# Half of a dense expert stage placed inside the second half of a four-layer recurrence, in a single-core Trainium2 kernel

## The chip, the core and the metric

The kernel runs on one core of a Trainium2 chip. The core has five engines that run side by side, each with its own program: TensorE (matmuls, written PE in the rows; PEld is its weight load), VectorE (DVE), ScalarE (ACT), GpSimd (POOL) and SyncE (SP, which here only issues DMAs). They meet only through semaphores: an instruction can wait for a count and raise one when it ends. SBUF is the working memory (128 partitions), PSUM the small memory into which TensorE writes; it has eight banks of 128x512 fp32. The metric is the time of one execution on the device, in microseconds (us); lower is better.

## The reference

All arithmetic is fp32. The tokens are 32 sequences of 128 tokens with 128 features. In short:

```python
# adapter: 10 languages, one per sequence, two small matrices, LayerNorm
x_a = layernorm(x + relu(x @ W1[id] + b1[id]) @ W2[id] + b2[id]) * gamma[id] + beta[id]
# four layers of a selective state space model, 256 channels, 16 states each
for layer in range(4):
    xs, z = split(layernorm(h) @ W_in.T)                 # 2 x 256 channels
    u = silu(causal_conv4(xs))
    dt, B, C = split(u @ W_x.T)                          # 8, 16, 16
    dt = softplus(dt @ W_dt.T + b_dt)
    for t in range(128):                                 # per channel and state
        H = exp(dt[t] * A) * H + dt[t] * B[t] * u[t]
        y[t] = sum over 16 states of H * C[t]
    h = h + ((y + u * Dp) * silu(z)) @ W_out.T
x1 = x + h
# dense stage: 8 weighted experts and one shared one, all of them for all tokens
dense = sum over 9 experts of w[e] * (silu(x1 @ Wg[e]) * (x1 @ Wu[e])) @ Wd[e]
# sparse stage: router, top 2 of 8, fixed capacity, gelu experts
out = x1 + sum of top-2 gate * expert(dense)
```

## The kernel before

The program has four phases that follow one another: `setup_phase` (adapter, weights), `mamba_phase` (the recurrence), `dense_phase` and `sparse_phase`. The change is about the second and third.

**Tiling of the recurrence.** Four sequences form a group (512 tokens); there are 8 groups and 4 layers. One group in one layer is called an *item* here; the 32 items are run layer by layer, all 8 groups in each. The 256 channels are two halves of 128 partitions, and the 16 states are worked two at a time, so that an item has 16 *steps* (8 pairs of states for each half). A step is a chain over four engines:

- ScalarE, `decay`, L543: two `exp` of 128x508 write a buffer `dA` (four of them);
- VectorE, `input_term`, L592: the product `psdB<-psU,Bt` of 128x1024, with `psU` (dt times u) in PSUM and `Bt` (the rows of B spread over the partitions) in SBUF, the result in one of two PSUM buffers;
- VectorE, `scan_step`, L598: the scan along time of 128x1024, `hh<-dA,psdB`, one input in SBUF and one in PSUM;
- GpSimd, `gg<-hh,Ct`, L683: the product with C of 128x1024, both inputs in SBUF;
- TensorE, `sum_states`, L385: two identity matmuls of 512 columns that add the two states to `psY`.

Beside the steps each engine's program has, at step numbers fixed by hand in the tables `PE_AT`, `ACT_AT`, `DVE_AT` and `POOL_AT`, the preparation of the next item and the finish of the one before: projections, convolution and time step (PE L416 to L429, ACT L486 to L517), `dt` and `dtu` on GpSimd (L653, L658, 128x1024 each), ScalarE's copies of `dtu` into `psU` (L522), the gates `yg` (GpSimd L668, 128x512 twice), the residual (GpSimd L664), and the LayerNorm statistics (VectorE L606 to L612, GpSimd L643 to L648).

**What sets the order.** Every engine runs its program in order. A scan may run four steps ahead of GpSimd (`NHB`), GpSimd four ahead of TensorE (`NGB`), the exps four ahead of the scan (`NDA`), the input terms one ahead of the scan (`NDB` is 2). PSUM is full: two buffers of two banks for the input term, two banks `psU`, one `psY`, one `psW` for all projections.

**The dense stage**, 8 groups one after another, has 36 rounds per group (9 experts, 4 pieces of the hidden layer). A round is three matmuls of 512 columns (L897, L901, L866), a Silu on ScalarE (L948) and a product on VectorE (L1051, one input in PSUM). GpSimd scales the input once per expert (L811). The input of a group is x + h, added on VectorE from two SBUF tensors (`residual`, L980). Router logits and slots of group g are computed inside group g+1.

## Time and profile before

| | us |
|---|---|
| three timed runs: median | 2933.65 |
| lowest and highest | 2931.76, 2934.94 |
| the profiled execution: its time | 2935.85 |
| its span, first to last instruction | 2934.1 |
| TensorE busy | 2515.8 (86%) |
| VectorE busy | 2104.9 (72%) |
| GpSimd busy | 1780.1 (61%) |
| ScalarE busy | 1456.5 (50%) |

The shares are averages over stages that have different limits, so they say little by themselves. A timeline row gives the start, the duration, engine, line, operation, output and inputs, and in brackets how long the engine had been idle before and who released it. Records of one matmul of 512 fp32 columns come in pairs (two records, one matmul).

### The profile page before, as it was taken

To read this page: it belongs to the slowest core of one execution; us is meant where nothing else is said; L and a number is where in the kernel's file an instruction comes from. 1 tells how busy PE (TensorE), PEld (TensorE's weight loads), DVE (VectorE), ACT (ScalarE), POOL (GpSimd) and SP (SyncE) were. 2 spreads that over 40 slices of the span, in tenths; PEclk is the share of its full clock that TensorE was granted. 3 is DMA by queue.
4 is the path that set the end of the run, shared out by engine and by line. 5 is a ranking of instruction groups with operands and counts; after the bars stand their busy time and mean duration, and the time that the engine had idled before them with its cause. 6 is when DMAs were issued, how large, how long until landed. Compare 5 with 4: busy or idle time off the path is not lost. (4 is left out here: it accounts for less than half of the span.)

```text
span 2934.1 us, 27727 instructions
## 1 busy us (share of the span) xinstructions
PE 2515.8 (86%) x6470; PEld 1112.9 (38%) x6470; DVE 2104.9 (72%) x2075; ACT 1456.5 (50%) x2337; POOL 1780.1 (61%) x1090
## 2 busy tenths in 40 slices
PE   5588888888888888888888888869999999999586
PEld 3233333333333333333333333324444444444264
DVE  4399999999999999999999999972333333333221
ACT  2366657666666665666566667632222222222222
POOL 3278887888888788888888887861022202221266
PEclk9798999999999999989999999999999999999798
DMA  7334533543453344345434533516000000000154
GB/s 204 139 128 179 201 127 144 194 170 127 170 197 139 136 185 186 127 157 196 154 128 174 205 127 142 195 61 220 8 15 8 15 7 11 25 8 1 45 111 70
DMA packets 130514, 354.33 MB, mean 121 GB/s; under 512 B 21716, under 2 KB 85410, under 8 KB 97570
## 3 DMA queue, kind: packets, MB, share of 16 engines
q1 hardware_dynamic: 116770, 342.46, 32.1%
q0 software_dynamic: 11264, 7.98, 1.8%
q10 hardware_dynamic: 2432, 3.38, 0.3%
q14 instruction: 34, 0.28, 0.0%
q8 instruction: 14, 0.23, 0.0%
HBM read 330.34 MB, written 23.99 MB: 121 GB/s over the span
## 5 line engine op out<-in xcount | busy, mean ns | idle before, releaser
L683 POOL TENSOR_TENSOR gg<-hh,Ct 128x1024 f32<-128x1024 f32 x512 | 1205.0, 2356 | 336.2 <-DVE hh L598 322.4
L598 DVE TENSOR_TENSOR_SCAN hh<-dA,psdB 128x1024 f32<-128x1024 f32 x512 | 1170.7, 2287 | 59.4 <-ACT dA L543 6.1
L385 PE MATMUL psY<-gg,ident 128*128 128x512 f32 x2048 | 1024.4, 636 | 128.0 <-POOL gg L683 127.7
L543 ACT ACTIVATE dA<-dt,Acur 128x508 f32<-128x508 f32 x1024 | 664.6, 707 | 14.9 <-DVE hh L598 14.4
L385 PEld LDWEIGHTS psY<-gg,ident 128*128 128x128 f32 x2048 | 390.9, 200 | 689.8 <-issue 420.6
L592 DVE TENSOR_TENSOR psdB<-psU,Bt 128x1024 f32<-128x1024 f32 x512 | 617.6, 1206 | 36.8 <-ACT psU L522 36.8
L1051 DVE TENSOR_TENSOR ac<-sg,d_bank 128x512 f32<-128x512 f32 x288 | 198.1, 688 | 514.0 <-PE d_bank L901 496.8
L948 ACT ACTIVATE sg<-d_bank 128x512 f32<-128x512 f32 x288 | 171.9, 597 | 534.6 <-PE d_bank L897 521.3
L811 POOL TENSOR_TENSOR xw<-x1T,wbc 128x512 f32<-128x512 f32 x72 | 74.9, 1041 | 568.1 <-PE d_bank L901 563.8
L897 PE MATMUL d_bank<-x1T,wgu 128*128 128x512 f32 x576 | 296.6, 597 | 1.9 <-DMA wgu<-in_Wu 1.9
L901 PE MATMUL d_bank<-xw,wgu 128*128 128x512 f32 x576 | 295.5, 595 | 0.0
L866 PE MATMUL d_bank<-ac,wdn 128*128 128x512 f32 x576 | 291.7, 593 | 0.0
L416 PE MATMUL psW<-xnT,wcur 128*128 128x512 f32 x512 | 235.9, 603 | 3.9 <-DMA diag<-diags_l 2.1
L493 ACT ACTIVATE u<-psW,parc 128x512 f32<-128x512 f32 x64 | 44.0, 687 | 240.1 <-PE psW L416 240.1
L901 PEld LDWEIGHTS d_bank<-xw,wgu 128*128 128x128 f32 x576 | 110.3, 191 | 138.6 <-issue 124.0
L866 PEld LDWEIGHTS d_bank<-ac,wdn 128*128 128x128 f32 x576 | 109.7, 190 | 137.5 <-issue 137.5
L897 PEld LDWEIGHTS d_bank<-x1T,wgu 128*128 128x128 f32 x576 | 108.5, 191 | 130.0 <-issue 130.0
L380 PE MATMUL psY<-u,diag 128*128 128x512 f32 x128 | 86.1, 760 | 74.0 <-ACT yg L528 74.0
L416 PEld LDWEIGHTS psW<-xnT,wcur 128*128 128x128 f32 x512 | 98.5, 193 | 131.4 <-issue 119.0
L429 PE MATMUL psW<-xd,wdcur 8*128 8x512 f32 x128 | 87.2, 766 | 63.5 <-ACT soft L511 43.4
L1127 POOL DMA_INDIRECT out<-eos,home x64 | 99.2, 1549 | 69.1 <-DVE eos L1219 50.2
L821 POOL DMA_INDIRECT disp<-tok,idx x64 | 62.5, 976 | 77.0 <-DVE idx L1029 50.3
...
## 6 DMA issues: line engine op xcount, KB each, us to landing
Bt<-rows SPq DMA_DIRECT2D x128, 1024.0 KB, 6.0
Ct<-rows SPq DMA_DIRECT2D x128, 1024.0 KB, 4.7
...
```

Of the source, the lines that this page charges most:

```text
L385: ins = pe.matmul(psY[:, :], lhsT=ident[:, :], rhs=gg[k % NGB][:, j, :], start=False, stop=(k % NK == NK - 1 and j == 1))
L416: ins = pe.matmul(psW[:, :], lhsT=wcur[:, k, c * 128:(c + 1) * 128], rhs=xnT[:, :, k:k + T], start=(k == 0), stop=(k == NTAP - 1))
L543: ins = act.activation(dA[k % NDA][:, j, :, 1:T], dt[p][:, c, :, 1:T], ACT.Exp, scale=Acur[p][:, s:s + 1])
L592: dve.tensor_tensor(dB[k % NDB][:, :, :], psU[c][:, :].unsqueeze(1).broadcast_to([128, 2, TOK]), Bt[:, s:s + 2, :], ALU.mult).then_inc(dbu, 1)
L598: dve.tensor_tensor_scan(out=hh[k % NHB][:, :, :].rearrange("p c t -> p (c t)"), data0=dA[k % NDA][:, :, :, :].rearrange("p c q t -> p (c ...
L683: pool.tensor_tensor(gg[k % NGB][:, :, :], hh[k % NHB][:, :, :], Ct[:, s:s + 2, :], ALU.mult).then_inc(prod, 1)
L866: ins = pe.matmul(psD[:, :], lhsT=wdn[:, r // NF, r % NF, :], rhs=ac[r % NAC][:, :], start=(r == 0), stop=(r == NST - 1))
L897: pe.matmul(psG[r % 2][:, :], lhsT=wgu[:, e, 0, f * 128:(f + 1) * 128], rhs=x1T[p][:, :, :], start=True, stop=True).then_inc(gated, 1)
L901: pe.matmul(psU[r % 2][:, :], lhsT=wgu[:, e, 1, f * 128:(f + 1) * 128], rhs=xw[(NE1 * p + e) % NXW][:, :, :], start=True, stop=True).then_ ...
L948: act.activation(sg[r % NSG][:, :], psG[r % 2][:, :], ACT.Silu).then_inc(silued, 1)
L1051: dve.tensor_tensor(ac[r % NAC][:, :], sg[r % NSG][:, :], psU[r % 2][:, :], ALU.mult).then_inc(acted, 1)
L1127: pool.indirect_dma_start(tokens, bass.IndirectOffsetOnAxis(ap=home[p][:, n:n + 1], axis=0), eos[p][:, n, :], None, bounds_check=NSEQ * T ...
```

## The change

The recurrence and the first half of the dense stage become one phase, `wave_phase`, written out without a hardware loop.

- **Order of items.** The first 16 items take groups 0 to 3 through all four layers, the last 16 take groups 4 to 7 (`layer`, `group`). From item 15 (`FIRST`) on, the dense stage of groups 0 to 3 is run inside the steps, nine rounds to an item: `G_AT`, `U_AT` and `D_AT` hold the steps at which TensorE issues the gate, up and down matmul of each; ScalarE copies a gate four or five steps later (`place_gate`) and runs the Silus together (`silu_gates`); VectorE's product follows the scan two steps behind the up matmul (`act_product`). TensorE transposes x1, GpSimd adds x and scales the inputs (`add_x`, `scale`).
- **Steps by pairs of states.** A step now alternates between the two halves of the channels for the same pair of states. `psY` has two banks, one for each half; the sums are copied and gated once per item as 128x1024.
- **PSUM.** The `psU` banks are gone: VectorE's input term reads `dtu` from SBUF. From item 14 on only one of the two input-term buffers is used as such (`dB[0]`); the other holds the gate and up results of the dense stage. The dense sum has a bank.
- **Input terms from GpSimd.** In items 0 to 13, GpSimd makes the input term of steps 4, 9 and 13 (`GIVEN`, `give`), and ScalarE moves it to PSUM (`move_given`).
- **Sums.** `PAIRED` is empty: TensorE adds all sixteen states. The residual is one more identity matmul in `out_projection`.
- The rest of the dense stage, groups 4 to 7, follows in `dense_phase`; the router's work for all 8 groups is done there, two groups in each (`posts`), as is the last group's at the end. The dispatch buffers are cleared early in the recurrence. `sparse_phase` keeps its work.

VectorE's program. Names ending in a digit are buffers; `psU0` is PSUM, `dtu0` and `Bt` are SBUF, `f_sg` is the Silu in SBUF. In the kernel before, two steps of the first item:

```order
L592 TENSOR_TENSOR psdB0<-psU0,Bt 128x1024 [waits m_scan,m_b_ld2]
L598 SCALAR_TENSOR_TENSOR hh0<-dA0,psdB0 128x1024 [waits m_prod,m_dbu,m_da]
L592 TENSOR_TENSOR psdB1<-psU0,Bt 128x1024 [waits m_scan]
L598 SCALAR_TENSOR_TENSOR hh1<-dA1,psdB1 128x1024 [waits m_prod,m_dbu,m_da]
L606 BN_STATS stats<-h_res 128x6 [waits m_moments]
```

And in the changed kernel, a stretch of an item in the second half:

```order
L730 TENSOR_TENSOR psdB0<-dtu0,Bt 128x1024 [waits m_scan,m_b_ld3]
L741 SCALAR_TENSOR_TENSOR hh2<-dA2,psdB0 128x1024 [waits m_prod,m_dbu,m_da]
L762 TENSOR_TENSOR f_ac0<-f_sg,psdB1 128x512 [waits m_downed,m_upped,m_sg_ok]
L730 TENSOR_TENSOR psdB0<-dtu0,Bt 128x1024 [waits m_scan]
L741 SCALAR_TENSOR_TENSOR hh3<-dA3,psdB0 128x1024 [waits m_prod,m_dbu,m_da]
L730 TENSOR_TENSOR psdB0<-dtu0,Bt 128x1024 [waits m_scan,m_b_ld0]
L741 SCALAR_TENSOR_TENSOR hh0<-dA0,psdB0 128x1024 [waits m_prod,m_dbu,m_da]
L762 TENSOR_TENSOR f_ac1<-f_sg,psdB1 128x512 [waits m_downed,m_upped,m_sg_ok]
```

The input term has both inputs in SBUF and always the same output buffer, so that its wait on `m_scan` is for the scan just before it; nine times per item a product of the dense stage stands between a scan and the next input term.

GpSimd's program in the first half. In the kernel before, the first eleven steps of the first item:

```order
L683 TENSOR_TENSOR gg<-hh,Ct 128x1024 x7
L643 TENSOR_TENSOR vare<-mv,eps 128x4
L644 TENSOR_SCALAR negm<-mv 128x4
L646 TENSOR_TENSOR rstd<-vare,nhalf 128x4
L648 TENSOR_TENSOR nmr<-negm,rstd 128x4
L683 TENSOR_TENSOR gg<-hh,Ct 128x1024 x4
```

In the changed kernel, the same eleven steps:

```order
L818 TENSOR_TENSOR gg<-hh,Ct 128x1024
L810 TENSOR_TENSOR f_sg<-dtu,Bt 128x1024
L818 TENSOR_TENSOR gg<-hh,Ct 128x1024 x5
L810 TENSOR_TENSOR f_sg<-dtu,Bt 128x1024
L818 TENSOR_TENSOR gg<-hh,Ct 128x1024
L784 TENSOR_TENSOR vare<-mv,eps 128x4
L785 TENSOR_SCALAR negm<-mv 128x4
L787 TENSOR_TENSOR rstd<-vare,nhalf 128x4
L789 TENSOR_TENSOR nmr<-negm,rstd 128x4
L818 TENSOR_TENSOR gg<-hh,Ct 128x1024 x2
L810 TENSOR_TENSOR f_sg<-dtu,Bt 128x1024
L818 TENSOR_TENSOR gg<-hh,Ct 128x1024 x2
```

Three products of 128x1024 (`f_sg<-dtu,Bt`) have come to GpSimd in each item.

On TensorE, twenty-seven matmuls of 512 columns of the dense stage stand among the sums and projections of an item of the second half.

The diff, cut to its core:

```diff
-NK = NS // 2
-NSTEP = NH * NK
-NCK, CKS = 4, NS // 4
+NSTEP = NS
+ROUND = NG // 2
+NB = NE1
+NDF = NG // 2
+FIRST = NL * ROUND - 1
...
+GIVEN = {4: 0, 9: 5, 13: 8}
+POOL_AT = {3: ["gate"], 6: ["rstd"], 10: ["dt"], 11: ["dtu"]}
+G_AT = [-9, -8, -6, -5, -4, -3, -2, -1, 3]
+U_AT = [6, 8, 9, 11, 12, 14, 15, 19, 20]
+D_AT = [10, 10, 11, 13, 14, 18, 18, 21, 22]
+PAIRED = []
...
+def layer(t):
+    return t // ROUND % NL
+def group(t):
+    return t // (NL * ROUND) * ROUND + t % ROUND
+def stream(at, i, k):
+    return [NB * v + m for v in range(NDF * NF) for m in range(NB) if NSTEP * (FIRST + v) + at[m] == NSTEP * i + k]
...
-        psU = [ctx.enter_context(nc.psum_tensor(f"psU{c}", [128, TOK], f32)) for c in range(NH)]
-        psY = ctx.enter_context(nc.psum_tensor("psY", [128, TOK], f32))
+        psG, psU = dB[1][:, 0, :], dB[1][:, 1, :]
+        psY = ps("psY", [128, NH, TOK])
+        psD = ps("psD", [128, TOK])
...
                 def input_term(i, k):
-                    n, c, s = NSTEP * i + k, k // NK, 2 * (k % NK)
...
-                    at_least(dve, scan, CR + n + 1 - NDB)
-                    dve.tensor_tensor(dB[k % NDB][:, :, :], psU[c][:, :].unsqueeze(1).broadcast_to([128, 2, TOK]), Bt[:, s:s + 2, :], ALU.mult).then_inc(dbu, 1)
+                    n, c, s = NSTEP * i + k, k % NH, k // NH
...
+                    if assisted(i, k):
+                        return
+                    b, free = (k % NDB, n + 1 - NDB) if i < FIRST - 1 else (0, n)
+                    at_least(dve, scan, free)
+                    dve.tensor_tensor(dB[b][:, :, :], dtu[i % 2][:, c, :].unsqueeze(1).broadcast_to([128, 2, TOK]), Bt[:, s % NPR, :, :], ALU.mult).then_inc(dbu, 1)
...
+                def act_product(n):
+                    dve.wait_ge(sg_ok, n // NB + 1)
+                    dve.wait_ge(upped, n + 1)
+                    at_least(dve, downed, n - 1)
+                    dve.tensor_tensor(ac[n % 2][:, :], sg[:, n % NSLG, :], psU, ALU.mult).then_inc(acted, 1)
...
+                        input_term(i, k)
+                        scan_step(i, k)
+                        for n in stream([a + 2 for a in U_AT], i, k):
+                            act_product(n)
...
+                def give(i, k):
...
+                    pool.tensor_tensor(given[helped(n) % 2], dtu[i % 2][:, c, :].unsqueeze(1).broadcast_to([128, 2, TOK]), Bt[:, s % NPR, :, :], ALU.mult).then_inc(gave, 1)
...
+                def move_given(i, k):
...
+                    act.activation(dB[k % NDB][:, :, :], given[helped(n) % 2], ACT.Copy).then_inc(moved, 1)
...
+                def place_gate(n):
+                    act.wait_ge(gated, use_g(n) + 1)
...
+                    act.activation(sg[:, n % NSLG, :], psG, ACT.Copy).then_inc(gfree, 1)
...
+                def gate(n):
...
+                    pe.wait_ge(gfree, use_g(n))
+                    pe.matmul(psG, lhsT=fwg[:, e % NXW, f * 128:(f + 1) * 128], rhs=flat(n // NST), start=True, stop=True).then_inc(gated, 1)
...
+                def up(n):
...
+                    at_least(pe, acted, n)
+                    pe.matmul(psU, lhsT=fwu[:, e % NXW, f * 128:(f + 1) * 128], rhs=xw[:, e % NXW, :, :].rearrange("p q t -> p (q t)"), start=True, stop=True).then_inc(upped, 1)
+                def down(n):
...
+                    pe.wait_ge(acted, n + 1)
...
+                    pe.matmul(psW[:, :], lhsT=ident[:, :], rhs=flat(group(t)), start=True, stop=False)
...
+                def scale(a):
+                    d, e = a // NE1, a % NE1
+                    pool.wait_ge(gfree, use_t(d) + 1)
+                    at_least(pool, upped, NF * (a - NXW + 1))
+                    pool.tensor_tensor(xw[:, e % NXW, :, :], residents(d), wbc[:, e, G * d:G * (d + 1)].unsqueeze(2).broadcast_to([128, G, T]), ALU.mult).then_inc(scaled, 1)
```

## Rows read from the trace of the kernel before

**Rows 1.** Windows: busy us of each engine (count), TensorE clock, DMA, by phase
```profile
core 0: us, PE busy (x) PEld busy (x) DVE busy (x) ACT busy (x) POOL busy (x), PEclk, DMA share, GB/s
123.25:1965.46 1842.21, 1558.30 (x3657) 634.86 (x3658) 1781.44 (x1303) 1173.30 (x1863) 1501.77 (x791) 0.93 0.42 159
1965.46:2740.00 774.54, 764.13 (x1891) 347.77 (x1890) 243.09 (x508) 204.83 (x333) 136.29 (x167) 0.99 0.10 32
2740.00:2934.10 194.10, 130.15 (x726) 92.63 (x724) 40.03 (x95) 46.02 (x72) 106.93 (x72) 0.87 0.44 83
```

**Rows 2.** Costliest groups by line, with shape: busy us, mean ns, idle before
```profile
L683 POOL TENSOR_TENSOR gg<-hh,Ct 128x1024 f32<-128x1024 f32 x512 | 1205.0, 2356 | 336.2 <-DVE hh L598 322.4 <-PE psY L385 13.8
L598 DVE TENSOR_TENSOR_SCAN hh<-dA,psdB 128x1024 f32<-128x1024 f32 x512 | 1170.7, 2287 | 59.4 <-ACT dA L543 6.1 <-DVE psdB L592 5.9 <-POOL gg L683 5.5
L592 DVE TENSOR_TENSOR psdB<-psU,Bt 128x1024 f32<-128x1024 f32 x512 | 617.6, 1206 | 36.8 <-ACT psU L522 36.8
L980 DVE TENSOR_TENSOR x1g<-xin,h_res 128x512 f32<-128x512 f32 x8 | 7.5, 936 | 3.2 <-DMA xin<-in_x 3.2
```

**Rows 3.** Timeline of VectorE, two steps in the middle of the recurrence
```profile
998.61 2.29 DVE L598 TENSOR_TENSOR_SCAN hh<-dA,psdB 128x1024 f32<-128x1024 f32 x1
1000.81 1.21 DVE L592 TENSOR_TENSOR psdB<-psU,Bt 128x1024 f32<-128x1024 f32 x1
1002.11 2.29 DVE L598 TENSOR_TENSOR_SCAN hh<-dA,psdB 128x1024 f32<-128x1024 f32 x1
```

**Rows 4.** Timeline of GpSimd: `deviation`, a step beside rows 3, back-to-back work
```profile
329.30 0.20 POOL L643 TENSOR_TENSOR vare<-mv,eps 128x4 f32<-128x4 f32 x1
...
331.03 2.36 POOL L683 TENSOR_TENSOR gg<-hh,Ct 128x1024 f32<-128x1024 f32 x1
...
1001.05 2.35 POOL L683 TENSOR_TENSOR gg<-hh,Ct 128x1024 f32<-128x1024 f32 x1 [1.15 <-DVE hh L598]
...
1030.15 2.35 POOL L683 TENSOR_TENSOR gg<-hh,Ct 128x1024 f32<-128x1024 f32 x1 [1.14 <-DVE hh L598]
1032.46 2.35 POOL L653 TENSOR_TENSOR dt<-dt,soft 128x1024 f32<-128x1024 f32 x1
```

**Rows 5.** Timeline: the residual add on VectorE, GpSimd idle, then GpSimd busy
```profile
1977.89 0.69 DVE L980 TENSOR_TENSOR x1g<-xin,h_res 128x512 f32<-128x512 f32 x1 [3.17 <-DMA xin<-in_x]
...
2085.77 1.04 POOL L811 TENSOR_TENSOR xw<-x1T,wbc 128x512 f32<-128x512 f32 x1 [9.26 <-PE d_bank L901]
2085.78 0.69 DVE L1051 TENSOR_TENSOR ac<-sg,d_bank 128x512 f32<-128x512 f32 x1 [1.78 <-PE d_bank L901]
2086.39 0.97 DVE L980 TENSOR_TENSOR x1g<-xin,h_res 128x512 f32<-128x512 f32 x1
```

**Rows 6.** Timeline of the setup: a VectorE product between two GpSimd products
```profile
17.55 0.72 POOL L167 TENSOR_TENSOR taps<-wraw,cwb 128x256 f32<-128x256 f32 x1
17.65 0.89 DVE L216 TENSOR_TENSOR wbc<-wbc 128x256 f32<-128x256 f32 x1
18.23 0.90 POOL L167 TENSOR_TENSOR taps<-wraw,cwb 128x256 f32<-128x256 f32 x1
```

**Rows 7.** Timeline of the setup: VectorE beside back-to-back GpSimd products
```profile
26.19 1.40 POOL L167 TENSOR_TENSOR taps<-wraw,cwb 128x256 f32<-128x256 f32 x2
26.33 1.46 DVE L235 SCALAR_TENSOR_TENSOR ad_nrm<-ad_y,ad_mv,ad_gb 128x128 f32<-128x128 f32 x1
```

**Rows 8.** Timeline of the setup: VectorE beside GpSimd's power on four elements
```profile
55.74 0.62 DVE L235 SCALAR_TENSOR_TENSOR ad_nrm<-ad_y,ad_mv,ad_gb 128x128 f32<-128x128 f32 x2
55.76 1.01 POOL L174 TENSOR_TENSOR ad_rstd<-ad_vare,nhalf 128x4 f32<-128x4 f32 x1
```

**Rows 9.** Windows: one item of the recurrence, one group of the dense stage
```profile
1000.00:1057.60 57.60, 50.67 (x118) 20.76 (x117) 55.83 (x42) 37.06 (x59) 47.31 (x25) 0.91 0.42 161
2086.39:2181.25 94.86, 94.86 (x237) 43.24 (x236) 30.97 (x68) 25.84 (x42) 17.37 (x18) 1.00 0.04 12
```

**Rows 10.** Timeline of TensorE late in the dense stage: two matmuls
```profile
2734.57 1.02 PE L897 MATMUL d_bank<-x1T,wgu 128*128 128x512 f32 x2
2735.43 1.02 PE L901 MATMUL d_bank<-xw,wgu 128*128 128x512 f32 x2
```

More of the change, by code:

```diff
@@ new lines, in wave_phase @@
+        fwg = sb("f_wg", [128, NXW, F])
+        fwu = sb("f_wu", [128, NXW, F])
+        fwd = sb("f_wd", [128, NXW, NF, D])
+        xw = sb("f_xw", [128, NXW, G, T])
+        xin = sb("f_xin", [128, G, D])
+        ac = [sb(f"f_ac{b}", [128, TOK]) for b in range(2)]
+        given = [sg[:, 2 * b:2 * b + 2, :] for b in range(2)]
+        zrow = sg[:, 4:7, :].rearrange("p s t -> p (s t)")[:, 0:NCH * RW]
+        dB = [ps(f"psdB{b}", [128, 2, TOK]) for b in range(NDB)]
+        psG, psU = dB[1][:, 0, :], dB[1][:, 1, :]
@@ L318, in at_least, with assisted, helped, residents @@
+        b_ld, c_ld = ([sem(f"{n}_ld{j}") for j in range(NPR)] for n in "bc")
+        g_ld, ud_ld = ([sem(f"{n}_ld{j}") for j in range(NXW)] for n in ("fg", "fud"))
+        W = psw_uses()
+        def assisted(i, k):
+            return i < FIRST - 1 and k in GIVEN
+        def helped(n):
+            return sum(assisted(a // NSTEP, a % NSTEP) for a in range(n))
         def at_least(eng, sm, v):
-            if not (isinstance(v, int) and v <= CR):
+            if v > 0:
                 eng.wait_ge(sm, v)
+        def residents(d):
+            return h_res[:, G * d:G * (d + 1), :]
@@ new lines, in sum_states, with out_projection @@
+                def sum_states(i, k):
+                    n = NSTEP * i + k
+                    pe.wait_ge(prod, n + 1)
+                    last = 1 if i >= FIRST and k in PAIRED else 2
+                    for j in range(last):
+                        ins = pe.matmul(psY[:, k % NH, :], lhsT=ident[:, :], rhs=gg[k % NGB][:, j, :], start=False, stop=(k >= NSTEP - NH and j == last - 1))
+                    ins.then_inc(red, 1)
+                def out_projection(t):
+                    pe.wait_ge(ygated, t + 1)
+                    pe.wait_ge(wfree, W["out", t])
+                    pe.matmul(psW[:, :], lhsT=ident[:, :], rhs=flat(group(t)), start=True, stop=False)
@@ L454, in last, with transpose_x @@
                     for q in range(G):
                         for c in range(NH):
-                            ins = pe.matmul(psW[:, q * T:(q + 1) * T], lhsT=yg[1][:, c, q * T:(q + 1) * T], rhs=wo[:, (NL - 1) * NH + c, :], start=(c == 0), stop=(c == NH - 1))
+                            ins = pe.matmul(psW[:, q * T:(q + 1) * T], lhsT=yg[:, c, q * T:(q + 1) * T], rhs=wo[:, layer(t) * NH + c, :], start=False, stop=(q == G - 1 and c == NH - 1))
                     ins.then_inc(wready, 1)
-                loop(pe, body, first, last)
+                def transpose_x(d):
+                    pe.wait_ge(x1_ok, d + 1)
+                    if d == 0:
+                        pe.wait_ge(scan, NSTEP * (FIRST - 1))
+                    at_least(pe, gfree, use_t(d))
+                    for q in range(G):
+                        ins = pe.transpose(psG[:, q * T:(q + 1) * T], h_res[:, G * d + q, :], ident[:, :])
+                    ins.then_inc(gated, 1)
@@ new lines, in down @@
+                def down(n):
+                    e, f = expert(n)
+                    pe.wait_ge(acted, n + 1)
+                    if n % NST == 0:
+                        at_least(pe, sum_ok, n // NST)
+                    pe.matmul(psD[:, :], lhsT=fwd[:, e % NXW, f, :], rhs=ac[n % 2][:, :], start=(n % NST == 0), stop=(n % NST == NST - 1)).then_inc(downed, 1)
+                transposes(0)
+                for k in sorted(PE_AT):
+                    for what in PE_AT[k]:
+                        if what in PRE:
+                            pre(0, what)
@@ L575, in _ @@
+                            if what == "sums" and i > 0:
+                                copy_sums(i - 1)
+                        decay(i, k)
+                copy_sums(NIT - 1)
+                added(NIT - 1)
             @block.vector
             def _(dve):
-                for sm in (dbu, scan, stat, moments):
-                    dve.sem_inc(sm, CR)
                 for b in range(NDA):
                     ins = dve.memset(dA[b][:, :, :, 0:1], 0.0)
-                ins.then_inc(zeroed, 1)
@@ L753, in at_least, with posts, sums @@
                 eng.wait_ge(sm, v)
-        def loop(eng, first, body, last):
-            first()
-            body(0, 0, False, True)
-            with eng.Fori(0, NG // 2 - 1) as j:
-                body(2 * j + 1, 1, True, True)
-                body(2 * j + 2, 0, True, True)
-            body(NG - 1, 1, True, False)
-            last(NG - 1, 1)
+        def posts(h, r, at):
+            return [2 * h + j for j in range(2) if 2 * h + j < NG - 1 and r == P_AT[j] + at]
+        def sums(g):
+            return h_res[:, G * g:G * (g + 1), :]
         with nc.Block() as block:
```

852 lines of the change are left out of this document (451 added, 401 removed).

## The prediction

> **What bounds the kernel now.** I read the windows by phase first, then the groups by line, then the timelines of VectorE and GpSimd inside one step. In the recurrence, 123.25 to 1965.46, 1842.2 us for 32 items or 57.57 us each, VectorE is busy 1781 of 1842 us and GpSimd 1502 [rows 1]. VectorE's share is the sum of two rows of 512 instructions each, the scan with 2.287 us and the input term with 1.206 us [rows 2]. In the timeline a step starts 3.50 us after the last one (998.61 to 1002.11) with no idle between: the input term starts 0.09 us before the scan's recorded end, the next scan 0.09 us behind the input term [rows 3]. 16 steps make 56.0 us; 1.6 us remain for the statistics. GpSimd's product starts 0.15 us after the scan that it needs (scan ends 1000.90, product starts 1001.05) [rows 3, 4]. So VectorE sets the recurrence. The dense stage, 774.5 us, is TensorE's: one group takes 94.86 us with TensorE busy all through [rows 9], 0.86 us per matmul of 512 columns (2734.57 to 2735.43) [rows 10]. What is to be gained is four of eight such groups: 379 us.
>
> **The rows that decide the price.** The input term now reads two tensors in SBUF; before, one of its inputs was in PSUM, as for the scan. What such a VectorE instruction does beside GpSimd the trace shows in three places. (a) The residual add of 128x512, both inputs in SBUF, takes 0.69 us with GpSimd idle. When GpSimd's product of two SBUF tensors is in work (2085.77 to 2086.81), it takes 0.97 us and ends 0.55 us behind GpSimd's end, while GpSimd keeps its 1.04 us [rows 5]. The mean of all eight, 0.936 us [rows 2], is one of 0.69 and seven of 0.97. 512 elements need about 0.52 us of data: 1024 take 1.206 us [rows 2] and 512 take 0.69 [rows 5], which is 1.01 ns per element. So it moved nothing until GpSimd was done. (b) In the setup a product of 256 elements that starts 0.10 us behind a GpSimd product takes 0.89 us where its data need 0.26 us; it ends 0.27 us after that product's end, and the next GpSimd product takes 0.90 instead of 0.72 us [rows 6]. So the second of the two waits in either direction, and GpSimd's loss is the data time less 0.08 us. (c) Once VectorE was passed over: its product of 128 elements waited 1.46 us across the boundary of two back-to-back GpSimd products [rows 7].
>
> The Trainium skill, "SBUF — State Buffer", section "SBUF: two separate sides", says that the port pair shared by VectorE and GpSimd is an exclusive lock, taken by whichever starts first for the whole instruction, and names VectorE instructions with two SBUF inputs. The trace agrees [rows 5, 6]. "For the whole instruction" isn't quite what the trace shows [rows 8]: two VectorE instructions with two SBUF inputs ran at 0.31 us each inside a GpSimd instruction of 1.01 us on four elements. If a GpSimd product lost the whole 1.21 us of each input term and not its data time less 0.08, the sum below would be 45 us longer.
>
> **First half, items 0 to 13.** VectorE saves three input terms: 13 x 3.50 + 3 x 2.20 + 1.6 = 53.7 us without any blocking. GpSimd: 16 products, 3 given input terms, gate, dt and dtu, all 128x1024, 22 x 2.31 us (1030.15 to 1032.46) = 50.8, and 1.73 for the deviation (329.30 to 331.03) [rows 4]: 52.5 us. But each of the 13 input terms stops GpSimd for 1.04 - 0.08 = 0.96 us, together 12.5 us: 65.0 us in which one or the other moves data. The input term is issued ahead of the scan's end and gets in first; the queue of four `hh` buffers lets GpSimd fall behind, then the scans wait for it. I take 66 us; 53.7 if nothing is blocked. 14 items: 924 us.
>
> **Second half, items 15 to 30.** Per step VectorE now waits for its own scan before the input term: 2.29 + 0.09 + 1.21 + 0.09 = 3.68 us instead of 3.50. The dense product (0.69, next start 0.61 later [rows 5]) reads PSUM and SBUF and isn't blocked itself. But it puts the input term 0.61 us behind its place: GpSimd's product, released 0.15 us after the scan, is then in work and holds the port until 0.15 + 2.35 = 2.50 us; the input term's data (1.04, and 0.03 to its end) follow, then 0.09 and the scan: 2.50 + 1.07 + 0.09 + 2.29 = 5.95 us. Nine steps of an item are like that. In the seven others the two are released by the same scan, VectorE after 0.09 us and GpSimd after 0.15; I take it that VectorE gets in first, and GpSimd's product runs beside the next scan. 9 x 5.95 + 7 x 3.68 = 79.3 us. The statistics follow a product step and hide under GpSimd's 2.35. GpSimd's other work fits beside a scan in product steps; the gate after step 3 doesn't, 2.0 us, and about half of the 2.25 scalings per item, 1.5 us together. 82.8; with a little for late up matmuls, 83.5 us. 16 items: 1336.
>
> TensorE in such an item: 50.7 us of busy time now [rows 9] and 27 x 0.86 = 23.2: 73.9 us, under 83.5, so the dense matmuls cost only by the waits that they bring. They are issued behind the sums of their step, two steps ahead of VectorE's product; behind a late one wait the input term and the scan, with 1.9 us of slack, since the input term waits for GpSimd anyhow. ScalarE: 37.1 us [rows 9], nine gate copies and their Silus, about 10: 47. Neither is near.
>
> Item 14 (no dense products, no given terms): 16 x 3.68 + 10 for gate, dt, dtu, statistics and the x add = 69. Item 31: four product steps, 4 x 5.95 + 12 x 3.68 + 2 = 70.
>
> **Rest.** Before the recurrence 123.3, unchanged. Behind it 968.6 now (774.5 + 194.1) [rows 1], less 4 x 94.86, and 4 more posts of the router on TensorE at some 2 us: 597.6. DMAs: the same bytes of B and C in pieces of half the size, with a lead of six steps, over 20 us; the weights of an expert (three loads per 4 rounds) have ten steps. I cost them at nothing; if one came late it would show as a VectorE wait at the first step of a pair.
>
> Sum: 123.3 + 924 + 69 + 1336 + 70 + 597.6 = 3120 of span. The profiled execution was 1.8 us longer than its span and 2.2 above the median, so the median is about the span: 3120. Some passing over as in (c) will happen: I say 3130 us, 196 slower. The recurrence grows by 2399 - 1842 = 557 us to save 371.
>
> **Rivals.**
> 1. *Nothing of weight is blocked.* The input term keeps 1.21 us though both inputs are in SBUF. First half 53.7; second half by VectorE 16 x 3.68 + 1.6 + 9 x 0.61 = 66, by TensorE 67 at full clock to 74: 71. 123.3 + 14 x 53.7 + 62 + 16 x 71 + 62 + 597.6 = 2733. For it: the design, in which GpSimd takes over products, needs it. Against: the seven adds of [rows 2, 5]. 10 in 100.
> 2. *GpSimd gets in first also in the plain steps, or back to back.* The 0.06 us between the releases [rows 3, 4] is smaller than what is unknown of when each asks for the port. Then all steps of the second half take 5.95: 95.2 x 18 = 1714 us for items 14 to 31 instead of 1475, and 3360. If instead it passes VectorE over in the first half as in [rows 7], each of the six extra products costs 4.4 instead of 2.3 us and leaves the port idle under the next scan: 80 instead of 66, and 3330. For: [rows 7]. Against: [rows 6], where VectorE got in. 27 in 100 for 3230 to 3450.
> 3. *Blocking is partial*, or GpSimd is mostly out of the way when the input term comes, because TensorE delays the products past the 2.35 us and GpSimd has finished: nine steps at 4.6 to 5 us, 70 to 75 per item, 2900 to 3040. 13 in 100, a quarter of it below 2928.
> 4. *TensorE decides*: its clock falls in the new waits and 73.9 becomes 90 and more; then VectorE waits in every product step, at 3200 and up. Part of the 27.
>
> The other side begins where the second half's items cost less than 83.5 - 196/16 = 71 us with the first half as forecast: that needs the product steps at 4.6 us.
>
> **How the numbers follow.** Main case 50 in 100, 3040 to 3230; rival 1 10, rival 3 13, rivals 2 and 4 27. The range 2960 to 3400 leaves out rival 1 and the lower half of rival 3, and a few in 100 above. A measurement of this kernel tells 0.2% (6 us) from no change: faster 0.13, within 0.2% 0.01, slower 0.86.
>
> **What would show it.** In the changed profile the rows of `psdB<-dtu,Bt` have a mean well above 1.21 us: near 2 in the first half, 2.5 to 3 behind a dense product. GpSimd's `gg<-hh,Ct` has a mean above 2.6. VectorE's busy share stays near 95% while the step is longer: the wait is inside the instruction and not in front of it. A step of the second half alternates between 3.7 and 5.95 us. The dense group of the last phase stays at some 97 us. It is wrong if `psdB<-dtu,Bt` keeps 1.21 us (rival 1), if no step of the second half is near 3.7 (rival 2), or if VectorE's product waits for the up matmul for over 2 us in most steps (rival 4).

## The result and the profile after

The changed kernel takes 3238.06 us (median of 4 runs, 3236.67 to 3241.4), the kernel before 2933.16 (4 runs beside it): the ratio is 1.1041, 95% interval 1.1022 to 1.106, so it is 305 us slower. Forecast were 3130 us with a range of 2960 to 3400: the sign and the range hold, the size was too small by 108 us. 3238 us is 8 us above the band of the prediction's main case (3040 to 3230), inside the one that it gave to its rivals 2 and 4.

The costliest groups of the changed kernel by line, the same three that stand in [rows 2] (busy us, mean ns, idle time before and its releaser):

```profile
L818 POOL TENSOR_TENSOR gg<-hh,Ct 128x1024 f32<-128x1024 f32 x512 | 1415.8, 2770 | 592.6 <-DVE hh L741 585.2
L741 DVE TENSOR_TENSOR_SCAN hh<-dA,psdB 128x1024 f32<-128x1024 f32 x512 | 1166.0, 2284 | 122.5 <-ACT dA L657 84.4
...
L730 DVE TENSOR_TENSOR psdB<-dtu,Bt 128x1024 f32<-128x1024 f32 x470 | 1087.5, 2314 | 47.4 <-POOL dtu L799 36.1
```

The scan has kept its 2.28 us. The input term has gone from 1206 to 2314 ns and GpSimd's product from 2356 to 2770, with next to no idle time ahead of the input term: the wait stands inside the instruction, and would be read as work. 512 input terms of 1.206 us were 618 us; 470 of 2.314 are 1088.

Windows of the changed kernel by phase, answering to [rows 1] (the stretch and its length, then busy us of PE, PEld, DVE, ACT and POOL with the number of instructions, the granted TensorE clock, the DMA share and GB/s). An item runs from the start of its first scan to the start of the next item's. The rows are: before the recurrence, items 0 to 13, item 14, items 15 to 30, item 31, the dense stage that is left, the sparse stage:

```profile
0.00:121.20 121.20, 61.44 (x196) 37.09 (x196) 40.33 (x170) 34.19 (x74) 36.20 (x62) 0.94 0.57 163
121.20:1077.30 956.10, 746.45 (x1633) 306.14 (x1634) 859.64 (x534) 545.84 (x830) 900.88 (x363) 0.87 0.44 147
1077.30:1154.00 76.70, 60.90 (x133) 24.89 (x132) 74.18 (x42) 38.48 (x61) 59.20 (x24) 0.87 0.42 139
1154.00:2558.70 1404.70, 1200.68 (x2737) 502.33 (x2736) 1338.38 (x788) 717.28 (x1059) 912.84 (x403) 0.94 0.38 126
2558.70:2636.30 77.60, 47.83 (x95) 19.01 (x95) 75.10 (x35) 17.80 (x27) 44.73 (x16) 0.84 0.18 61
2636.30:3041.00 404.70, 396.07 (x1011) 184.09 (x1012) 137.46 (x357) 114.98 (x181) 99.12 (x129) 0.98 0.11 35
3041.00:3236.50 195.50, 132.35 (x731) 93.52 (x729) 40.75 (x96) 46.64 (x73) 106.91 (x72) 0.88 0.43 82
```

The recurrence takes 2515 us (121.2 to 2636.3) where it took 1842; what follows it takes 600.2 where it took 968.6. So 368 us are saved behind the recurrence and 673 are paid in it.

Two timelines of the changed kernel in item 20, VectorE and then GpSimd (start, duration, engine, line, operation; in brackets the idle time before):

```profile
1687.68 0.66 DVE L762 TENSOR_TENSOR f_ac<-f_sg,psdB 128x512 f32<-128x512 f32 x1
1688.26 3.02 DVE L730 TENSOR_TENSOR psdB<-dtu,Bt 128x1024 f32<-128x1024 f32 x1
1691.38 2.29 DVE L741 TENSOR_TENSOR_SCAN hh<-dA,psdB 128x1024 f32<-128x1024 f32 x1
1693.70 1.23 DVE L730 TENSOR_TENSOR psdB<-dtu,Bt 128x1024 f32<-128x1024 f32 x1
1695.02 2.29 DVE L741 TENSOR_TENSOR_SCAN hh<-dA,psdB 128x1024 f32<-128x1024 f32 x1
1697.41 3.42 DVE L730 TENSOR_TENSOR psdB<-dtu,Bt 128x1024 f32<-128x1024 f32 x1
1700.92 2.29 DVE L741 TENSOR_TENSOR_SCAN hh<-dA,psdB 128x1024 f32<-128x1024 f32 x1
```

```profile
1687.84 2.35 POOL L818 TENSOR_TENSOR gg<-hh,Ct 128x1024 f32<-128x1024 f32 x1 [3.54 <-DVE hh L741]
1690.16 2.02 POOL L834 TENSOR_TENSOR f_xw<-h_res,wbc 128x512 f32<-128x512 f32 x1
1693.74 3.39 POOL L818 TENSOR_TENSOR gg<-hh,Ct 128x1024 f32<-128x1024 f32 x1 [1.57 <-DVE hh L741]
1697.39 2.35 POOL L818 TENSOR_TENSOR gg<-hh,Ct 128x1024 f32<-128x1024 f32 x1 [0.25 <-DVE hh L741]
```

All three cases are here. At 1688.26 the input term comes 0.42 us behind GpSimd's product, because the dense product stood in front of it, and takes 3.02 us; it ends 1.1 us behind GpSimd. At 1693.70 it starts 0.03 us behind the scan's end and 0.04 ahead of GpSimd: it takes 1.23 us, and GpSimd's product 3.39. At 1697.41 no product stood in front, and still it starts 0.10 us behind the scan's end (1697.31) and 0.02 behind GpSimd: 3.42 us. Scan to scan the three steps are 5.90, 3.64 and 5.90 us.

The difference between the last two is in the program. The first is the second half of a pair of states and waits for the scan alone (`m_scan`); the other opens a pair and waits for the rows of B as well (`m_scan,m_b_ld`), which had long been there. That wait costs some 0.07 us of start, and 0.07 us decides who gets in first, at 2.26 us of VectorE's time. It is so in the whole stretch of items 14 to 31. Of the input terms that come straight behind a scan, the 64 that wait for the scan alone start 0.02 to 0.04 us after its end, and 55 of them take 1.2 us; the 77 that wait for B as well and have nothing else in front of them start 0.09 to 0.14 us after it, and 67 of them take 3.4 us. Of the sixteen steps of item 20 only two are 3.64 us, one is 4.28 and one 5.61; the other twelve are 5.89 or more, though only nine have a product.

### The profile page after: what moved, and what is told of

Read it like the earlier page. It is cut to its first block and busy times, and to the rows that moved or that the text cites. A ratio compares the mean times of both kernels' runs of the same rounds, so it can differ in the third digit from the quotient of the medians.

```text
span 3236.5 us, 23204 instructions
## 1 busy us (share of the span) xinstructions
PE 2645.7 (82%) x6530; PEld 1167.1 (36%) x6530; DVE 2565.8 (79%) x2019; ACT 1515.2 (47%) x2304; POOL 2159.9 (67%) x1069
## 5 line engine op out<-in xcount | busy, mean ns | idle before, releaser
L818 POOL TENSOR_TENSOR gg<-hh,Ct 128x1024 f32<-128x1024 f32 x512 | 1415.8, 2770 | 592.6 <-DVE hh L741 585.2
L741 DVE TENSOR_TENSOR_SCAN hh<-dA,psdB 128x1024 f32<-128x1024 f32 x512 | 1166.0, 2284 | 122.5 <-ACT dA L657 84.4
L730 DVE TENSOR_TENSOR psdB<-dtu,Bt 128x1024 f32<-128x1024 f32 x470 | 1087.5, 2314 | 47.4 <-POOL dtu L799 36.1
L1206 DVE TENSOR_TENSOR ac<-sg,d_bank 128x512 f32<-128x512 f32 x144 | 99.0, 687 | 243.7 <-PE d_bank L1056 226.6
L483 PE MATMUL psW<-xnT,wcur 128*128 128x512 f32 x512 | 239.6, 611 | 8.3 <-DMA diag<-diags_l 6.5
L1105 ACT ACTIVATE sg<-d_bank 128x512 f32<-128x512 f32 x144 | 86.0, 597 | 261.7 <-PE d_bank L1052 261.6
L538 PE MATMUL psdB<-f_xw,f_wu 128*128 128x512 f32 x288 | 154.4, 618 | 35.3 <-DVE f_ac L762 35.3
L606 ACT ACTIVATE u<-psW,parc 128x512 f32<-128x512 f32 x64 | 44.0, 687 | 258.7 <-PE psW L483 161.7
L530 PE MATMUL psdB<-h_res,f_wg 128*128 128x512 f32 x288 | 161.5, 645 | 0.0
L483 PEld LDWEIGHTS psW<-xnT,wcur 128*128 128x128 f32 x512 | 100.7, 197 | 140.7 <-issue 132.0
L1052 PE MATMUL d_bank<-x1T,wgu 128*128 128x512 f32 x288 | 148.9, 599 | 0.7 <-ACT x1T L1083 0.7
L1056 PE MATMUL d_bank<-xw,wgu 128*128 128x512 f32 x288 | 147.9, 595 | 0.0
L1019 PE MATMUL d_bank<-ac,wdn 128*128 128x512 f32 x288 | 145.8, 592 | 0.0
L545 PE MATMUL psD<-f_ac,f_wd 128*128 128x512 f32 x288 | 143.6, 599 | 0.0
```

Source lines behind the costliest of these rows:

```text
L483: ins = pe.matmul(psW[:, :], lhsT=wcur[:, k, c * 128:(c + 1) * 128], rhs=xnT[:, :, k:k + T], start=(k == 0), stop=(k == NTAP - 1))
L530: pe.matmul(psG, lhsT=fwg[:, e % NXW, f * 128:(f + 1) * 128], rhs=flat(n // NST), start=True, stop=True).then_inc(gated, 1)
L538: pe.matmul(psU, lhsT=fwu[:, e % NXW, f * 128:(f + 1) * 128], rhs=xw[:, e % NXW, :, :].rearrange("p q t -> p (q t)"), start=True, stop=Tru ...
L545: pe.matmul(psD[:, :], lhsT=fwd[:, e % NXW, f, :], rhs=ac[n % 2][:, :], start=(n % NST == 0), stop=(n % NST == NST - 1)).then_inc(downed, 1)
L730: dve.tensor_tensor(dB[b][:, :, :], dtu[i % 2][:, c, :].unsqueeze(1).broadcast_to([128, 2, TOK]), Bt[:, s % NPR, :, :], ALU.mult).then_inc ...
L741: dve.tensor_tensor_scan(out=hh[k % NHB][:, :, :].rearrange("p c t -> p (c t)"), data0=dA[k % NDA][:, :, :, :].rearrange("p c q t -> p (c ...
```

## The experiments

Each runs on one chip beside the kernel before, whose median was 2936.3 to 2936.7 us. The theory under test (A) is that the time goes to the port that VectorE and GpSimd share for operands in SBUF, at a price that the order of arrival sets. The rivals, named in each expectation, are other things that came with the change: TensorE's order, ScalarE's late exps, the waits as such.

**1. The wait for B moved ahead.** The waits for the rows of B and for `dtu` are taken before the scan and not before the input term.

```diff
 def input_term(i, k):
-    if k == 0:
-        dve.wait_ge(dtu_ok, i + 1)
-    if c == 0:
-        dve.wait_ge(b_ld[s % NPR], 16 * (NS // 2 // NPR * i + s // NPR + 1))
...
 def scan_step(i, k):
+    if n + 1 < NSTEP * NIT:
+        inputs_ready((n + 1) // NSTEP, (n + 1) % NSTEP)
```

> Edit: VectorE waits for the piece of B (and, once per item, for dtu) in front of the scan before and no longer at the input term, so that the input term waits for the scan alone. Theory A (whoever asks first gets the shared SBUF port, and a second semaphore makes VectorE 0.07 us later than GpSimd): the plain steps that end ahead of an even-numbered input term and now take 5.90 us fall to 3.64; three per item in the second half, eight of item 14, three of item 31: 16 x 6.8 + 18 + 7 = 130 us less than 3238, 3108. First half unchanged within 1 us per item. Rival B (the steps of 5.90 come from something else, a late exp or a late TensorE): no change, 3238 within 10. Rival C (the wait merely moves its 0.07 us and the order stays): 3238 to 3250.

Measured: 3162.51 us (4 runs), 1.0772 of before [1.0754, 1.079], 76 us less than the changed kernel; theory A had expected some 130. The input term's mean falls to 1999 ns and GpSimd's product rises to 2908. Item 14, which has no dense products, falls from 76.7 to 69.0 us, exactly the forecast that had taken all plain steps as won. An item of the second half falls by 3.6 us only (87.8 to 84.2). The four plain steps ahead of an even-numbered input term are now 3.64 to 3.8 and give back 8.0 us of an item, but one or two steps of each item have become 7.7 to 10.1 us, and the idle time ahead of `f_ac` has grown from 33 to 90 us, 52 of it for `psD`. So the second wait is shown to decide the plain steps; in the second half over half of what they give back is lost again, and 3.6 us of an item are added waits for TensorE.

**2. The dense product moved behind the input term.** The order scan, dense product, input term becomes scan, input term, dense product.

```diff
                         input_term(i, k)
-                        scan_step(i, k)
-                        for n in stream([a + 2 for a in U_AT], i, k):
+                        for n in stream([a + 3 for a in U_AT], i, k):
                             act_product(n)
+                        scan_step(i, k)
```

> Edit: VectorE's product of the dense stage stands behind the next input term and ahead of its scan, and no longer between a scan and the next input term. Theory A (the product gives GpSimd the port first): the nine product steps of an item no longer hand the port to GpSimd by their place; they are then like plain steps, and only those whose input term waits for two semaphores still lose: about 8 x 3.64 + 8 x 5.9 + 9 x 0.6 + 1.2 = 83 us per item instead of 87.8, 3160. Rival B (the product steps are long because the up matmul is late): no gain or slower, since the product is asked for 1.2 us later at best; 3220 to 3260. Rival C (arrival order doesn't matter, VectorE gets in at once): 16 x 3.64 + 6.6 = 65, limited by TensorE at 74: 3238 - 16 x 14 = 3015.

Measured: 3127.53 us (4 runs), 1.0652 [1.0634, 1.067], 110 us less, where 78 were expected. No multiplication, byte or matmul is gone: only the place of nine instructions of 0.69 us per item.

**3. Both.**

> Both edits together. Theory A: all steps of the second half become plain steps that VectorE wins: 16 x 3.64 + 9 x 0.6 + 1.2 = 65 us per item for VectorE, less than the 67 to 74 of TensorE, so TensorE decides: 72 to 76 per item; 3238 - 16 x 14 - 20 for items 14 and 31: 2995 (2960 to 3040). The two gains are more than the sum of each alone (130 and 80). Rival B (TensorE or ScalarE hold the second half at over 83 already): the gain stays under 100 us, over 3130.

Measured: 3042.79 us (4 runs), 1.0366 [1.0348, 1.0383]: 195 us less, the sum of both (186) and a little more, and just outside the range expected (2960 to 3040). An item of the second half takes 77.3 us where the changed kernel has 87.8. Most of its steps are now 4.06 us with a product and 3.64 or 3.75 without; the 3.75 are those before whose scan the wait for B now stands, so the moved wait still costs 0.1 us there. The rest is five longer ones in most items, of 5.7 to 8.7 us in item 20. The rows of the two groups:

```profile
L726 DVE TENSOR_TENSOR psdB<-dtu,Bt 128x1024 f32<-128x1024 f32 x470 | 780.0, 1660 | 47.0 <-POOL dtu L805 37.6
...
L767 DVE TENSOR_TENSOR f_ac<-f_sg,psdB 128x512 f32<-128x512 f32 x144 | 98.0, 681 | 116.9 <-PE psD L545 70.9 <-PE psdB L538 46.0
```

**4. One operand back in PSUM, first half.** In items 0 to 14 VectorE's input term reads a constant in PSUM in place of `dtu`; this leaves `dtu` out of the recurrence of these items, and has the same instructions otherwise.

```diff
-dve.tensor_tensor(dB[b][:, :, :], dtu[i % 2][:, c, :].unsqueeze(1)...
+src = psD[:, :] if i < FIRST else dtu[i % 2][:, c, :]
+dve.tensor_tensor(dB[b][:, :, :], src.unsqueeze(1)...
```

> Edit: in items 0 to 14 the input term reads a constant in the PSUM bank that is free there, in place of dtu in SBUF; what it computes there is left out, its cost and all else is kept. Theory A (two SBUF inputs beside GpSimd): the input term is back at 1.21 us, GpSimd's products at 2.35; an item of the first half takes 53.7 to 56 us instead of 68.3, item 14 about 62; first half 14 x 13 = 180 us less, total near 3040. Rival B (SBUF operands are slower as such, or the given input terms and ScalarE's moves hold the first half): the item stays above 62 us.

Measured: 3123.97 us (one run). One line of the program, two prices, in one execution:

```profile
L731 DVE TENSOR_TENSOR psdB<-dtu,Bt 128x1024 f32<-128x1024 f32 x272 | 705.0, 2592 | 10.2 <-DVE hh L742 0.5
L731 DVE TENSOR_TENSOR psdB<-psD,Bt 128x1024 f32<-128x1024 f32 x198 | 239.4, 1209 | 37.1 <-POOL dtu L800 36.0
```

With one operand in PSUM the input term takes 1209 ns, as before; with both in SBUF 2592. GpSimd's input terms (`f_sg<-dtu,Bt`) take 2352 ns instead of 2695. Item 14 falls from 76.7 to 62.4 us and an item of the first half from 68.3 to 61.4, not to 54 to 56. The forecast of an unblocked item was 53.7 us. So of the 14.6 us over it 6.9 go with the second SBUF operand; the other 7.7 are something else. ScalarE's timeline shows what, and VectorE's behind it:

```profile
497.46 1.03 ACT L648 ACTIVATE psdB<-f_sg 128x1024 f32<-128x1024 f32 x1 [5.73 <-DVE hh L742]
498.42 1.01 ACT L638 ACTIVATE yg<-psY 128x1024 f32<-128x1024 f32 x1
503.00 0.69 ACT L606 ACTIVATE u<-psW,parc 128x512 f32<-128x512 f32 x1 [3.58 <-issue]
...
510.06 0.69 ACT L606 ACTIVATE u<-psW,parc 128x512 f32<-128x512 f32 x1 [5.16 <-PE psW L483]
510.65 1.31 ACT L657 ACTIVATE dA<-dt,Acur 128x508 f32<-128x508 f32 x2
```

```profile
508.32 1.21 DVE L731 TENSOR_TENSOR psdB<-psD,Bt 128x1024 f32<-128x1024 f32 x1
512.00 2.29 DVE L742 TENSOR_TENSOR_SCAN hh<-dA,psdB 128x1024 f32<-128x1024 f32 x1 [2.47 <-ACT dA L657]
```

ScalarE (first fence) stands idle for 5.73 us, because the move of a given input term into PSUM (L648) needs the buffer that the scan two steps back reads. It loses its lead of four steps with that. Without the lead its next long wait, 5.16 us for a projection of TensorE (L483), reaches the scan (second fence), which waits 2.47 us for its exps. Number 5 has such a wait of ScalarE as well (4.91 us ahead of L606), and the scans wait 2.5 us for exps there in all. For this part a rival holds, ScalarE's late exps, and not the port. The other rival, that an operand in SBUF is slower as such, is out: with both operands there and VectorE first the input term takes 1.23 us (1693.70 above).

**5. No given input terms.** `GIVEN = {}` in the changed kernel.

```diff
-GIVEN = {4: 0, 9: 5, 13: 8}
+GIVEN = {}
```

> Edit: GIVEN is empty, so that VectorE makes all sixteen input terms of an item and ScalarE moves none. The run before it showed an item of 61.4 us with no blocking at all, 7.7 over the sum of VectorE's instructions, with late exps: ScalarE's move of a given term waits for the scan two steps back and so gives up its lead of four steps. Theory A (port and ScalarE's lead): port time falls to 19 x 2.31 + 1.73 + 16 x 0.96 = 61 us, VectorE alone needs 16 x 3.5 + 1.6 = 57.6; an item of the first half takes 61 to 63 us instead of 68.3, 14 x 6 = 85 less: 3150. Rival B (GpSimd's help pays): three more input terms on VectorE, 3 x 1.2 to 3 x 3.4 us more per item, 72 and more: 3290.

Measured: 3224.06 us (one run), only 14 less, where 85 were expected. The scan's idle time for ScalarE falls from 84.4 to 2.5 us, but an item of the first half falls only from 68.2 to 66.1 in the mean, 29 us for the fourteen. The port takes back what ScalarE gives. (Items 15 to 30 are 11 us longer in this run, 88.5 against 87.8 us each; why is not known.) The three input terms that GpSimd had made stand on VectorE again. Most steps are 3.50 us, and some five of an item are 4.9 to 5.9, where GpSimd has instructions back to back or the statistics have made VectorE late; one place of the first kind:

```profile
467.07 3.24 POOL L818 TENSOR_TENSOR gg<-hh,Ct 128x1024 f32<-128x1024 f32 x1 [0.25 <-DVE hh L741]
470.29 2.35 POOL L804 TENSOR_TENSOR yg<-yg,sz 128x1024 f32<-128x1024 f32 x1
```

```profile
466.91 1.21 DVE L730 TENSOR_TENSOR psdB<-dtu,Bt 128x1024 f32<-128x1024 f32 x1
468.21 2.29 DVE L741 TENSOR_TENSOR_SCAN hh<-dA,psdB 128x1024 f32<-128x1024 f32 x1
470.41 3.31 DVE L730 TENSOR_TENSOR psdB<-dtu,Bt 128x1024 f32<-128x1024 f32 x1
```

VectorE won at 466.91, GpSimd's product became longer (3.24), so the gate behind it starts at 470.29, 0.12 us ahead of VectorE's next input term at 470.41, and this one pays 2.1 us. The expectation had some 6 us less for an item; it had counted what ScalarE stops costing, and of the port only the sum of its work.

**6. The kernel before, with its operand in SBUF.** ScalarE copies `dtu` to a tensor in SBUF and not to `psU`; all else is the kernel before.

```diff
-psU = [...nc.psum_tensor(f"psU{c}", [128, TOK], f32)...]
+uS = [sb(f"uS{c}", [128, TOK]) for c in range(NH)]
...
-dve.tensor_tensor(dB[k % NDB][:, :, :], psU[c][:, :]...
+dve.tensor_tensor(dB[k % NDB][:, :, :], uS[c][:, :]...
```

> Edit in the kernel before, and nothing else: ScalarE copies dtu into two SBUF tensors and not into PSUM, so that the input term has two SBUF inputs. Theory A (blocking): GpSimd has 16 products, dt, dtu, two gates, the residual and the deviation, 18 x 2.31 + 3 x 1.24 + 1.73 = 47 us, and loses 16 x 0.96: 62.4 us per item instead of 57.6; 32 x 4.8 = 155 us slower, 3090; the mean input term is over 1.6 us, gg over 2.9. Rival B (no blocking): the input term stays at 1.21, the time at 2936.

Measured: 3240.08 us (one run), 303 us or 10.3% over the kernel before, where 155 were expected. By this one edit an unchanged recurrence is as slow as the whole change. The items take 67.2 us instead of 57.5 (the first of them 65.2). The groups beside [rows 2]:

```profile
L683 POOL TENSOR_TENSOR gg<-hh,Ct 128x1024 f32<-128x1024 f32 x512 | 1607.8, 3143 | 201.6 <-DVE hh L598 201.0 <-PE psY L385 0.6
...
L592 DVE TENSOR_TENSOR psdB<-uS,Bt 128x1024 f32<-128x1024 f32 x512 | 921.5, 1800 | 36.8 <-ACT uS L522 36.8
```

The expectation had added what both engines need of the port (62.4 us an item). GpSimd is idle for 201 us, 6.3 an item, so the port is not in use all the time either: the loser's wait delays its own next instruction, and the sum of the port's work is a lower bound and not the price.

**7. Numbers 1, 2 and 5 together.**

> Edits: the moved wait, the product behind the next input term (together 3043) and GIVEN empty. Theory A: the two parts add, 3043 less 85 = 2958 (2940 to 2980), since one acts in items 15 to 31 and the other in 0 to 13. Rival B of the run without given terms: over 3080.

Measured: 3014.1 us (4 runs), 1.026 [1.0243, 1.0278]. Expected were 2958 (2940 to 2980), with 85 us for the given input terms; taking them out gives 29 us here. By items it is less than alone: the first half falls from 68.0 us in number 3 to 66.4, 22 us in all, against 29 in number 5. An item of the second half takes 77.0.

**8. Half of the operand in PSUM.** `psD` is not used by the dense stage before item 15. In items 0 to 14 ScalarE copies the first half of `dtu` into it, and every second input term reads it there.

```diff
+def place_half(i):
+    act.wait_ge(dtu_ok, i + 1)
+    at_least(act, dbu, NSTEP * i - 1)
+    act.activation(psD[:, :], dtu[i % 2][:, 0, :], ACT.Copy).then_inc(placed, 1)
...
+src = psD[:, :] if i < FIRST and c == 0 else dtu[i % 2][:, c, :]
```

> As the one before, and in items 0 to 14 ScalarE copies one half of dtu (128x512) into the PSUM bank that the dense sum uses only later; the eight even input terms of an item read it there. Theory A: only eight input terms stop GpSimd, 45.6 + 8 x 0.96 = 53.3 us of port, so VectorE with 57.6 decides: 58 to 59 us per item of the first half instead of 61 to 63, 15 x 3.5 = 50 less: 2905, which is below the kernel before. Rival B (ScalarE's copy costs its lead as the moves did): no gain, 2958 or more.

Measured: 2930.77 us (10 runs, 2929.0 to 2942.09), 0.9989 [0.9978, 1.0001]: no difference from before, and 83 us less than number 7. Items of the first half take 61.2 us, item 14 62.2. Expected was 2905, from a base of 2958 that number 7 had put at 3014. An item of the first half cost 2 to 3 us more than thought, and the gain was 83 us where 50 were expected, since without this edit it takes 66.4 us and not 61 to 63. The forecast came near by two misses that offset each other.

**9. A third buffer for the dense product**, since the idle time ahead of `f_ac` went to `psD` in number 3.

```diff
-ac = [sb(f"f_ac{b}", [128, TOK]) for b in range(2)]
+ac = [sb(f"f_ac{b}", [128, TOK]) for b in range(3)]
...
-at_least(dve, downed, n - 1)
+at_least(dve, downed, n - 2)
```

> This kernel is e8_half_in_psum with a third buffer for the dense product (f_ac: product n waits for down matmul n-2 and not n-1); one place fewer in f_sg pays for it. In e7 to e8 an item of the second half takes 77 us where the port alone would let it take about 72: steps of 4.1 with three of 5.4 to 8.7, and in e7 f_ac has 117 us of idle time ahead of it, put down to psD and psdB of TensorE. Theory A (what is left in the second half over the port is the wait for the two f_ac buffers, so TensorE's order of down matmuls): the idle time ahead of f_ac falls to under 40 us, an item of the second half takes 73 to 74 us, 16 of them save 50 to 60: 2875 us, 2% under the kernel before. Rival (the up matmul itself is late, or the exponentials of ScalarE, so that the third buffer only shows the next wait): 76 to 77 us an item and 2915 to 2931. First-half items stay at 61.2.

Measured: 2912.63 us (5 runs, 2911.61 to 2913.19), 0.9917 [0.9904, 0.9931] of the kernel before, so 0.8% faster than it and 10% faster than the changed kernel. The expected 2875 was missed, and the rival came true:

```profile
L778 DVE TENSOR_TENSOR f_ac<-f_sg,psdB 128x512 f32<-128x512 f32 x144 | 98.2, 682 | 80.6 <-PE psdB L538 73.5 <-issue 6.9
```

The wait for `psD` is gone and the one for the up matmul (L538) has grown from 46 us (number 3) to 73.5. An item takes 75.5 us, where number 8 has 76.6. Five of its steps are 5.7 to 7.1 us: in item 20 two of them hold a wait for the up matmul (1.75 and 1.93 us) and one a wait for ScalarE's exps (3.12). The other two are the port's again: input terms of 3.18 us behind back-to-back work of GpSimd, and of 2.43 us behind the statistics. What a step with a dense product is without such a wait shows in two others of the same item, GpSimd first and then VectorE:

```profile
1485.37 3.40 POOL L835 TENSOR_TENSOR gg<-hh,Ct 128x1024 f32<-128x1024 f32 x1 [0.36 <-DVE hh L757]
1489.43 3.39 POOL L835 TENSOR_TENSOR gg<-hh,Ct 128x1024 f32<-128x1024 f32 x1 [0.65 <-DVE hh L757]
```

```profile
1485.33 1.23 DVE L735 TENSOR_TENSOR psdB<-dtu,Bt 128x1024 f32<-128x1024 f32 x1
1486.47 0.68 DVE L778 TENSOR_TENSOR f_ac<-f_sg,psdB 128x512 f32<-128x512 f32 x1
1487.07 2.28 DVE L757 TENSOR_TENSOR_SCAN hh<-dA,psdB 128x1024 f32<-128x1024 f32 x1
1489.38 1.23 DVE L735 TENSOR_TENSOR psdB<-dtu,Bt 128x1024 f32<-128x1024 f32 x1
```

The same three instructions that took 5.90 us in the changed kernel take 4.06 (1487.07 to 1491.12, the next scan). GpSimd waits for the input term (3.40 instead of 2.35), and has the room for it; the dense product, which reads PSUM, runs meanwhile.

Two things could make the up matmul late in the long steps: TensorE's own work and order, or the scalings that it needs from GpSimd. The trace speaks for the first. Here are the two late matmuls (1471.46 and 1477.54) among what TensorE does before and between them, and the window of items 15 to 30:

```profile
1468.70 1.21 PE L530 MATMUL psdB<-h_res,f_wg 128*128 128x512 f32 x2
1469.74 1.88 PE L504 MATMUL psY<-gg,ident 128*128 128x512 f32 x4
1471.46 1.02 PE L538 MATMUL psdB<-f_xw,f_wu 128*128 128x512 f32 x2
...
1474.04 1.95 PE L513 MATMUL psW<-wo,yg 128*128 128x128 f32 x16
1475.82 1.88 PE L504 MATMUL psY<-gg,ident 128*128 128x512 f32 x4
1477.54 1.02 PE L538 MATMUL psdB<-f_xw,f_wu 128*128 128x512 f32 x2
```

```profile
1044.60:2252.30 1207.70, 1142.15 (x2732) 495.46 (x2731) 1055.80 (x788) 717.80 (x1065) 1013.32 (x404) 0.95 0.46 147
```

No idle time stands ahead of either, and all up matmuls together waited 0.9 us, none of it for a scaling. TensorE is busy for 1142 of 1208 us (95%) at a granted clock of 0.95: with the port's part mostly gone, it is near its own bound. No kernel with another order of TensorE was run, so how much of the wait is order and how much is amount stays open.

## Why the prediction was right, and where its size was off

| part | forecast us | measured us | off |
|---|---|---|---|
| before the recurrence | 123.3 | 121.2 | -2 |
| items 0 to 13 | 924 | 956.1 | +32 |
| item 14 | 69 | 76.7 | +8 |
| items 15 to 30 | 1336 | 1404.7 | +69 |
| item 31 | 70 | 77.6 | +8 |
| the rest | 597.6 | 600.2 | +3 |
| sum | 3120 | 3236.5 | +117 |

The forecast number had 10 us for passing over, so 108 are left between the medians.

- **The mechanism held.** That the input term without its PSUM operand pays, and only beside GpSimd, is shown by numbers 4 and 6, each the edit of one operand: 1209 against 2592 ns in one kernel, and 303 us in a kernel that has nothing else of the change. Rival 1 (nothing blocked, 2733) needed 1.21 us everywhere and has fallen. The signs came as named: the input term has a mean of 1.92 us in items 0 to 13 and 2.59 in items 15 to 30, GpSimd's product 2.77, and VectorE is busy for 1338 of 1405 us (95%) in items 15 to 30. Only the alternation of 3.7 and 5.95 us did not: twelve of the sixteen steps in item 20 are 5.89 us or more. GpSimd's loss to an input term, priced at 0.96 us, is 1.04 (3.39 against 2.35).
- **The product step** was forecast with 5.95 us and is 5.89 to 5.92 where nothing else waits; the nine of an item sum to 53.5 us in the mean of items 16 to 30, where 53.6 were forecast. That it is a matter of place was confirmed by number 2.
- **The plain step** was forecast with 3.68 and is 3.64 where VectorE gets in first. The term that was mis-sized is the seven of these, 7 x 3.68 = 25.8 us: they sum to 34.6. The prediction took all seven as won, since VectorE is released 0.06 us before GpSimd. It had named this margin as smaller than what it knew, in rival 2, but overlooked that every second input term waits for two semaphores, which was in the listing of the change. The four plain steps ahead of an even-numbered input term are 5.5 to 5.9 us in the mean, 8.0 us more than forecast; the other three are 0.8 more. The forecast's allowance of 4.2 us for the gate, the scalings and late matmuls was largely not needed, and hid half of the miss: 79.3 + 8.0 + 0.8 = 88.1 us measured, against 83.5. In items 14 and 31, with little else in them, the same term is +8 each, and both are back at 69 us with number 1.
- **Rival 2** thus came true in part, and 3238 us lies in the band that it had (3230 to 3450), not in that of the main case. Its other branch, 80 us an item in the first half, did not come. That the number still came as near as 108 us is partly the allowance's luck.
- **The first half** had 66 us and takes 68.3. Its sum was of port time, with the scans waiting for GpSimd. They did not: in 121.2 to 1065.8 VectorE waited ahead of its scans for ScalarE's exps (83.9 us, in 52 waits) and never for GpSimd. The port's part stands inside the input terms (thirteen of 1.92 instead of 1.21 us, 9.3 us an item), beside 6.0 us an item for exps. Number 4 shows that only 6.9 of the 14.6 us over the unblocked item go with the operand, the rest with ScalarE's lost lead behind the given input terms, which the prediction did not have at all. It had nearly the right sum for a partly wrong reason. The two do not simply add: with the given terms gone (number 5) an unblocked item would be 16 x 3.50 + 1.6 = 57.6 us, and it takes 66.1.
- **Rival 4** (TensorE decides) did not come: TensorE was busy for 1201 of 1405 us in items 15 to 30, and ahead of `f_ac` VectorE was idle for 33 us in all. TensorE comes near to being the bound only when the port's part is removed (117 us of idle time there in number 3, and TensorE busy for 95% in number 9).
- **Beyond the port**, the dense work on its new place does pay: behind the recurrence 368 us are saved of 371 forecast, and in number 9 the recurrence (125.7 to 2313.3) is 345 us longer than before, so that 26 of them are left.
